# Reordering a kernel's prologue, its third group of maxima, a PSUM bank and one result store

## The chip, the cores and the metric

One core of one Trainium2 chip runs the kernel. The metric is the device time in microseconds (us) of one execution; a kernel's time is the median of its runs.

## The reference

The input is `x`, 2 sequences of 1024 tokens with 256 features. Four residual layers follow one another, each on a layer-normalised `x`:

1. sliding-window attention: 32 heads of 8 features, window 128, softmax over 256 keys, an output product;
2. an FFN, 256 to 1024 to 256 with relu, whose weights are 4-bit codes times a scale per 64 columns, plus a rank-16 product (LoRA); weights are shared with layer 4;
3. a block with q, k, v through causal convolutions of 4 taps and two silus, unit-length q and k, a delta-rule scan over the tokens with an 8x8 state for each head, an output product, then a gated MLP, 256 to 704 to 256;
4. the FFN again.

```python
x = x + attn_a(layernorm(x))          # softmax(q k^T / sqrt(8)) v, window 128
x = x + ffn(layernorm(x))             # relu(x w_up + b) w_down + b, w = (code-7.5)*scale + A B
x = x + attn_b(layernorm(x))          # S = S - beta (S k - v) k^T per token; then silu(gate) * up @ Wdown
x = x + ffn(layernorm(x))
```

## The kernel before

The 1024 tokens are cut into 8 blocks of 128 (both sequences side by side: 256 columns). The program is one stream for each engine, written out by hand and joined by semaphores. Nothing is planned by a tool: the order of calls in each engine's `body` is the order of the work.

**Software pipeline.** `body(t)` works on three blocks at once: block n = t+1 (attention, first FFN and the inputs of layer 3, called `following`), block t (the scan, `scan`) and block s = t-1 (gated MLP and second FFN, `tail`). `front` means that block n+1 is prepared too: its norm, its q and k, its maxima. `body(-1)` has neither scan nor tail, `body(0)` no tail, bodies 1 to 5 have everything, body 6 has no `front`. Then `last_scan` and a body with only a tail.

**Attention.** Each block has 32 units of 2 heads, in four groups (g) of 8. Scores are computed twice: `scores_max` (L1576) makes them in banks 1 and 2 for VectorE's row maxima (`max_unit`, L1053), `max_pieces` splits the maxima into three bf16 pieces, `turn_max` (L1605) transposes them, and ScalarE's `max_rows` (L705) writes them by DMA into the stacked queries. `scores` (L1616) then yields scores less the maximum, `exp_of` (L713) the exponentials, `values` (L1641) the product with v. The stacks (q in three bf16 pieces, k likewise, a row of maxima, a pad row) come from DRAM by SyncE's `load_stacks` (L397), 7 DMAs for a group, in a ring of three slots. For a block, maxima of groups 0 to 2 are made in the body before, those of group 3 in its own attention (`PASS1`, L54), with `turn_max(n, 3)` at unit `TURN_AT` (L59).

**FFN stretch.** After the attention, TensorE has the wo product, gate and up products of block s (`gate_up` L1788, banks 4 and 7 in turn, `late_bank`), the FFN of block n (`ffn_up`, `ffn_down`), the maxima of group 2 of block n+1, then `mlp_down` (L1801), beta and delta inputs of block n (`turn_a(n,3)`, `beta_in`, `delta_in`), and `ffn_c_up`/`ffn_c_down` of block s. VectorE's side: `act_of` (L1315, gate times up) between scan steps, `second_residual` (L1104), the maxima, `second_sums` (L1297, the scan's output, which SyncE stores), `third_residual` (L1324, needs `mlp_down`), convolutions, `products` (L1161), `result` (L1333), which SyncE stores and which frees bank 5 for `values` of the next block. The next body begins with `til_first` (L1180), which waits for three DMAs of q, k and v lanes.

**Prologue.** SyncE, ScalarE and GpSimd each issue loads in the order written. ScalarE has codes, scales and LoRA factors ahead of its first compute. SyncE has the constants, all layer weights, and then the stores of the q and k pieces. VectorE dequantises both FFN weights. TensorE waits for every weight, then makes the maxima of three groups, then enters `body(-1)`.

## Time and profile before

| | us |
|---|---|
| median of 3 runs (lowest, highest) | 1237.23 (1232.9, 1240.89) |
| the profiled execution | 1245.38 |
| its span | 1243.5 |

| engine | busy us | share of the span |
|---|---|---|
| TensorE matmul (PE) | 1010.6 | 81% |
| weight load (PEld) | 720.0 | 58% |
| VectorE (DVE) | 901.1 | 72% |
| ScalarE (ACT) | 520.6 | 42% |
| GpSimd (POOL) | 75.1 | 6% |

Mean granted TensorE clock: 0.904 of full. The chain of work that ended last is 36% DVE, 33% PE, 11% ACT, 7% DMA, 6% issue and 5% SyncE's queue. No engine is full; which of them ends a stage has to be read stage by stage. A busy share says how much of a stretch the engine had something in it, not that it set the end.

### The profile page before, as it was taken

The numbers are of one execution on the slowest core, as the hardware profiler recorded it, in microseconds if no ns is written. First come the engines' busy times: TensorE is split into PE (matmuls) and PEld (weight loads), VectorE is DVE, ScalarE is ACT, GpSimd is POOL, SyncE is SP. The second block draws the span as 40 slices with busy tenths as digits, with TensorE's granted clock in tenths as the row PEclk, the third lists the DMA queues.
The fourth block names the chain that finished last, engine by engine and source line by source line (L and its number), as shares of the span: only waits on it lengthen the run. The fifth ranks groups of instructions, "written<-read, shape, count | busy, mean of one in ns | idle before, by whom it ended". The sixth has DMA issues, their size and how long they took to land.

```text
span 1243.5 us, 24387 instructions
## 1 busy us (share of the span) xinstructions
PE 1010.6 (81%) x9880; PEld 720.0 (58%) x9880; DVE 901.1 (72%) x2297; ACT 520.6 (42%) x1075; POOL 75.1 (6%) x107
## 2 busy tenths in 40 slices
PE   3488778777988998889888997899888978866567
PEld 2256645554566766666666665676665656744445
DVE  2733377897889778887888786977888687967911
ACT  2034255326542655336532663364533644531122
POOL 2200000000000010001000010000000100010000
PEclk9579979986998999989999998999999989987768
DMA  9823013303420144013411242014300300020000
GB/s 281 154 42 75 22 59 82 57 1 96 85 43 1 43 112 75 2 35 95 81 22 35 78 80 40 1 46 110 75 1 27 95 3 1 18 77 1 1 25 9
DMA packets 94129, 67.90 MB, mean 55 GB/s; under 512 B 47744, under 2 KB 86848, under 8 KB 94016
## 3 DMA queue, kind: packets, MB, share of 16 engines
q1 hardware_dynamic: 88544, 60.75, 20.6%
q10 hardware_dynamic: 4960, 5.54, 1.7%
q8 instruction: 78, 1.28, 0.5%
q14 instruction: 35, 0.29, 0.1%
q0 software_dynamic: 512, 0.05, 0.1%
HBM read 45.57 MB, written 20.32 MB: 53 GB/s over the span
## 4 chain that ended last, share of the span: by engine, by line
DVE 36%; PE 33%; ACT 11%; DMA 7%; issue 6%; SPq 5%; POOL 1%; ACTq 0%; DVEq 0%; POOLq 0%
PE bank L1651 5%; PE bank L1805 4%; DVE state L1268 4%; DVE u_l L1255 4%; DVE state L1260 4%; DVE lane_buf L1246 4%; PE bank L1631 3%; PE bank L1748 3%; DMA q_l<-lane_q 3%; DVE lane_buf L351 3%; DVE mx L1056 2%; PE bank L1540 2%; DVE hid L1209 2%; DVE til L1210 2%; PE bank L1599 2%
## 5 line engine op out<-in xcount | busy, mean ns | idle before, releaser
L715 ACT ACTIVATE probs<-bank 128x512 f32<-128x512 f32 x256 | 152.2, 597 | 165.7 <-PE bank L1636 165.1
L1651 PE MATMUL bank<-probs,v_ext 128*9 128x128 f32 x2048 | 165.5, 284 | 16.1 <-ACT probs L715 6.9
L1056 DVE TENSOR_REDUCE mx<-bank 128x2 f32<-128x320 f32 x256 | 118.5, 485 | 53.8 <-PE bank L1599 48.6
L1594 PE MATMUL bank<-edge_mask,identb 128*32 128x128 bf16 x1024 | 81.8, 240 | 63.1 <-DVE mx L1056 43.0
L1796 PE MATMUL bank<-feat_c,wgu 128*128 128x256 f32 (+1 forms) x384 | 100.3, 414 | 26.7 <-DVE hid_c L1321 21.1
L1651 PEld LDWEIGHTS bank<-probs,v_ext 128*9 128x9 f32 x2048 | 91.0, 93 | 44.6 <-issue 21.9
L1631 PE MATMUL bank<-q_stack,k_stack 128*128 128x128 bf16 x1024 | 106.1, 229 | 8.6 <-DMA q_stack<-m_rows 7.9
L1599 PE MATMUL bank<-k_stack,q_stack 128*32 128x160 bf16 x2048 | 108.1, 256 | 0.0
L1796 PEld LDWEIGHTS bank<-feat_c,wgu 128*128 128x128 f32 (+1 forms) x384 | 74.0, 198 | 48.4 <-DVE hid_c L1321 24.7
L1631 PEld LDWEIGHTS bank<-q_stack,k_stack 128*128 128x128 bf16 x1024 | 62.4, 100 | 56.9 <-issue 28.4
L1594 PEld LDWEIGHTS bank<-edge_mask,identb 128*32 128x32 bf16 x1024 | 37.7, 97 | 92.6 <-DVE mx L1056 65.9
L1246 DVE TENSOR_TENSOR lane_buf<-state,til 128x128 f32<-128x128 f32 x256 | 74.7, 292 | 16.6 <-POOL lane_buf L603 10.2
L1268 DVE TENSOR_REDUCE state<-state 128x32 f32<-128x160 f32 x256 | 81.4, 318 | 7.2
L1255 DVE TENSOR_REDUCE u_l<-lane_buf 128x16 f32<-128x144 f32 x256 | 77.1, 301 | 7.0
L1260 DVE TENSOR_TENSOR state<-u_l,k_l 128x128 f32<-128x128 f32 x256 | 74.7, 292 | 7.6
L1723 PE MATMUL bank<-feat,w_up 128*128 128x256 f32 x256 | 66.4, 410 | 5.4 <-ACT feat L677 5.4
L1819 PE MATMUL bank<-feat_c,w_up 128*128 128x256 f32 x256 | 65.5, 406 | 5.1 <-ACT hid_c L861 3.7
L1540 PE MATMUL bank<-w_dn,hid 128*128 128x256 f32 x256 | 59.1, 390 | 8.0 <-ACT hid L780 8.0
L1134 DVE SCALAR_TENSOR_TENSOR conv<-raw,conv_w,conv 128x256 f32<-128x256 f32 x144 | 63.4, 482 | 2.6
L1636 PE MATMUL bank<-tri_mask,identb 128*32 128x128 bf16 x1024 | 62.6, 235 | 0.0
L1599 PEld LDWEIGHTS bank<-k_stack,q_stack 128*32 128x32 bf16 x2048 | 61.9, 103 | 0.6
L1819 PEld LDWEIGHTS bank<-feat_c,w_up 128*128 128x128 f32 x256 | 50.0, 202 | 20.9 <-ACT hid_c L861 6.2
(169 smaller groups left out, 1732.7 us busy)
## 6 DMA issues: line engine op xcount, KB each, us to landing
k_pieces<-conv SPq DMA_DIRECT2D x48, 128.0 KB, 2.3
k_stack<-k_pieces SPq DMA_DIRECT2D x32, 192.0 KB
k_stack<-k_pieces SPq DMA_DIRECT2D x32, 128.0 KB
k_l<-lane_k SPq DMA_DIRECT2D x8, 512.0 KB, 3.7
q_l<-lane_q SPq DMA_DIRECT2D x8, 512.0 KB, 5.7
q_pieces<-conv SPq DMA_DIRECT2D x24, 128.0 KB, 2.0
q_stack<-q_pieces SPq DMA_DIRECT2D x32, 96.0 KB
tok<-in_x SPq DMA_DIRECT2D x8, 256.0 KB, 3.2
```

The lines of the kernel that those rows point to most:

```text
L715: act.activation(probs[:, u % 2], score_bank[u % 2][:], ACT.Exp, scale=float(DK) ** -0.5).then_inc(exp_done, 1)
L1056: dve.tensor_reduce(mx[:, g, 2 * v:2 * v + 2], bank[1 + u % 2][:].rearrange("p (h k) -> p h k", h=2)[:, :, 0:SPAN], AX.X, ALU.max).then_in ...
L1246: at = mark(dve.tensor_tensor(first[:, c, :, :, 0:DK].rearrange("p v i (k e) -> p i v k e", e=2), state[:, c, :, :, C:C + 2].rearrange("p ...
L1255: at = mark(dve.tensor_reduce(u_l[:, c], first[:, c], AX.X, ALU.add))
L1260: at = mark(dve.tensor_tensor(products_of(c), u_l[:, c].rearrange("p v (o i) -> p v o i", o=1).broadcast_to([128, VR, DK, C]), kc[:, c:c + ...
L1268: at = mark(dve.tensor_reduce(state[:, c + 1, :, :, C:C + 2], state[:, c].rearrange("p v k (e j) -> p v k e j", e=2), AX.X, ALU.add))
L1594: pe.matmul(pb[rows].rearrange("p (h e t) -> p h e t", h=2, e=2)[:, :, :, 0:SUB], identb[:, rows], edge_mask[:].rearrange("p (o e t) -> p ...
L1599: last = pe.matmul(pb[s * SUB:(s + 1) * SUB, hp * 2 * W:hp * 2 * W + SPAN], q_stack[:, r, 2 * v + hp, s * SUB:(s + 1) * SUB], keys_of(r, 2 ...
L1631: last = pe.matmul(pb[:, at:at + W], keys_of(r, 2 * v + hp)[:, kb * W:(kb + 1) * W], q_stack[:, r, 2 * v + hp, :], start=(hp == 0 and kb = ...
L1651: last = pe.matmul(bank[5][row:row + VE, col:col + W], v_ext[:, b, kb, h, :], probs[:, u % 2, (hp * 2 + kb) * W:(hp * 2 + kb + 1) * W], st ...
L1796: last = pe.matmul(late_bank[i % 2][0:m, g * BT:(g + 1) * BT], wgu[:, k, g * INTER + 128 * i:g * INTER + 128 * i + m], fc[:, k], start=(k ...
L1819: last = pe.matmul(late_bank[i % 2][:, 0:BT], w_up[:, k, i * 128:(i + 1) * 128], fc[:, k], start=(k == 0), stop=(k == KT - 1))
```

## The change

- **Loads.** Codes and scales go from ScalarE's to SyncE's queue, the up half right behind the constants, the down half behind the pad stores. LoRA factors: up ones on SyncE, down ones on ScalarE. `ones`, `head_sum`, `to_lanes` join the layer weights, and these and `load_residual(0)` come after the stacks, `load_x(1)` and the landing of the first two groups' maxima. q pieces are stored from ScalarE's queue, k pieces from SyncE's; the pad rows are loaded from GpSimd's. Waits for `weights_in` move from the prologue to the first use (`relu_a(0,0)`, the wo product, `delta_weights`).
- **Prologue compute.** TensorE makes the LoRA up product first, ahead of the first transpose. VectorE clears `k_stack` first, dequantises the up weights in the prologue, adds the down part later; ScalarE copies the LoRA down product out of PSUM. The norm weights are multiplied in behind `first_apply(0)`.
- **Third group.** The prologue makes the maxima of groups 0 and 1 only; those of group 2 of block 0 are made in units 2 to 5 of the first attention, two a unit, with `turn_max` at unit 7.
- **Gates.** The six gate tiles use banks 4, 7, 3, 4, 7, 4; tile 2 waits for nothing, tile 3 for act 1, tile 4 for act 2, tile 5 for act 4.
- **Down product.** `mlp_down` is cut by sequence; two maxima tiles, half, two tiles, half, four tiles. VectorE's `second_sums` moves ahead of the last four of these maxima.
- **Small ones.** `TURN_AT` 20 to 19. `result` before `products(n, 1)`. `til_first` waits for the k and v lanes only, ScalarE's `queries_out` for the q lanes.

```diff
-TURN_AT = 20
+TURN_AT = 19
+THIRD_AT = 2
+        gate_bank = (bank[4], bank[7], bank[3], bank[4], bank[7], bank[4])
+        GATE_FREE = {3: 1, 4: 2, 5: 4}
...
@@ SyncE
             load_x(0)
+            for dst, src in [(lora_a_up, a["lora_a_up"]), (lora_b_up, a["lora_b_up"])]:
+                sp.dma_start(dst, src).then_inc(lora_up_in, 16)
             for dst, src in consts:
                 sp.dma_start(dst, src).then_inc(consts_in, 16)
+            quantised(q_up, a["q_up"], s_up, a["s_up"], KT, up_in)
             sp.wait_ge(zeroed, 1)
...
-            load_residual(0)
-            pieces_to_dram(0)
+            quantised(q_dn, a["q_dn"], s_dn, a["s_dn"], FT, dn_in)
+            first_keys()
             sp.wait_ge(pieces_out, 144)
             sp.wait_ge(pad_out, 48)
             sp.wait_ge(stack_init, 2)
             for g in range(RING):
                 load_stacks(0, g)
-                load_pad(0, g)
-            sp.wait_ge(tok_next_ready, 1)
             load_x(1)
+            for g in range(2):
+                sp.wait_ge(m_in[g], 16)
+            load_residual(0)
+            for dst, src in plain:
+                sp.dma_start(dst, src).then_inc(weights_in, 16)
...
@@ GpSimd
+            pool.wait_ge(stack_init, 2)
+            for r in range(RING):
+                load_pad(pool, 0, r, first_pads)
@@ ScalarE, attention
+                    if n == 0 and u == THIRD_AT + 5:
+                        max_rows(0, 2)
@@ VectorE
-                dve.wait_ge(lanes_in, n * 48 + 48)
+                dve.wait_ge(lanes_in, n * 32 + 32)
...
                 if front:
-                    for u in range(2 * UPG + 2, 3 * UPG):
+                    for u in range(2 * UPG + 2, 2 * UPG + 4):
+                        max_unit(n + 1, u)
+                if has_scan:
+                    second_sums(step)
+                if front:
+                    for u in range(2 * UPG + 4, 3 * UPG):
                         max_unit(n + 1, u)
                     max_pieces(n + 1, 2)
-                if has_scan:
-                    second_sums(step)
...
                     products(n, 0)
-                    products(n, 1)
                 if tail:
                     result(s)
+                if following:
+                    products(n, 1)
...
+            zero = mark(dve.memset(k_stack[:], 0.0))
             norm_next_vars(0)
@@ TensorE
+                    if n == 0 and THIRD_AT <= u < THIRD_AT + 4:
+                        for v in range(2):
+                            scores_max(0, 2 * UPG + 2 * (u - THIRD_AT) + v)
...
-                if i >= 2:
-                    pe.wait_ge(act_ready, n * IT + i - 1)
+                if i in GATE_FREE:
+                    pe.wait_ge(act_ready, n * IT + GATE_FREE[i])
...
-                if front:
-                    for v in range(2 * UPG, DONE_EARLY * UPG):
-                        scores_max(n + 1, v)
-                if tail:
-                    mlp_down(s)
+                for b in range(B):
+                    if front:
+                        for v in range(2 * UPG + 2 * b, 2 * UPG + 2 * b + 2):
+                            scores_max(n + 1, v)
+                    if tail:
+                        mlp_down(s, b)
+                if front:
+                    for v in range(2 * UPG + 4, DONE_EARLY * UPG):
+                        scores_max(n + 1, v)
...
+            pe.wait_ge(lora_up_in, 32)
+            for k in range(KT):
+                for c in range(2):
+                    last = pe.matmul(bank[2 * k + c][:], lora_a_up[:, k * 128:(k + 1) * 128],
+                                     lora_b_up[:, c * 512:(c + 1) * 512], start=True, stop=True)
+            last.then_inc(up_prod, 1)
             pe.wait_ge(early_in, 16 * (len(early) + 2))
             turn_next(0)
```

## Rows read from the trace of the kernel before

**Rows 1.** Stretches: us, busy us (instructions) of PE, PEld, DVE, ACT, POOL, granted clock, DMA share, GB/s.

```profile
0.00:40.00 40.00, 20.13 (x54) 13.36 (x55) 17.65 (x15) 8.34 (x14) 12.78 (x19) 0.92 1.05 285
52.00:73.00 21.00, 12.23 (x291) 6.67 (x291) 13.71 (x40) 0.52 (x2) 0.00 (x0) 0.50 0.45 57
```

**Rows 2.** Timeline of the prologue: start us, us, engine, line, operation, count, [idle before, releaser].

```profile
13.42 2.12 ACT L963 COPY wqkv_a<-hid 128x512 f32<-128x512 f32 x2 [11.40 <-issue]
18.73 5.90 PE L1553 MATMUL bank<-feat_c,wqkv_a 128*128 128x256 f32 x16 [0.77 <-ACT feat_c L669]
28.69 5.11 SPq L431 DMA_DIRECT2D k_pieces<-conv  x2
30.23 4.05 PE L1904 MATMUL bank<-hid_c,u_l 16*128 16x512 f32 x8 [0.80 <-ACT v_ext L701]
```

**Rows 3.** Timeline of the prologue: stacks of group 0, first maxima, pieces of group 1, attention.

```profile
41.81 0.33 SPq L400 DMA_DIRECT2D q_stack<-in_zero_rows  x1
52.46 0.30 PE L1594 MATMUL bank<-edge_mask,identb 128*32 128x128 bf16 x4 [11.35 <-DMA k_stack<-in_pad_row]
60.45 0.30 PE L1594 MATMUL bank<-edge_mask,identb 128*32 128x128 bf16 x4 [3.54 <-DMA k_stack<-in_pad_row]
65.48 0.17 DVE L1065 TENSOR_SCALAR mpieces<-mx 128x16 bf16<-128x16 f32 x1
73.57 0.59 PE L1631 MATMUL bank<-q_stack,k_stack 128*128 128x128 bf16 x4 [0.54 <-DMA q_stack<-m_rows]
```

**Rows 4.** GpSimd's groups up to 60 us: line, operation, count, busy us, mean ns, idle before.

```profile
L552 POOL DMA_DIRECT2D k_stack<-k_stack x12 | 6.1, 514 | 0.0
```

**Rows 5.** DMA issues of the whole run: target and source, queue, count, KB each, us to landing.

```profile
q_l<-lane_q SPq DMA_DIRECT2D x8, 512.0 KB, 5.7
sqk<-lane_v SPq DMA_DIRECT2D x8, 256.0 KB, 3.9
```

**Rows 6.** Timeline of body 1: the wo product and gate tile 2, columns as in Rows 2.

```profile
362.83 1.89 PE L1540 MATMUL bank<-wo_a,feat 128*128 128x256 f32 x8
...
373.54 2.61 PE L1796 MATMUL bank<-feat_c,wgu 128*128 128x256 f32 x8 [1.98 <-DVE hid_c L1321]
```

**Rows 7.** Timeline of body 1: the second residual, maxima, sums, down product.

```profile
400.08 0.69 DVE L1110 TENSOR_TENSOR x<-bank,x_in 128x512 f32<-128x512 f32 x1 [0.88 <-PE bank L1540]
402.38 0.24 PE L1594 MATMUL bank<-edge_mask,identb 128*32 128x128 bf16 x4 [1.84 <-DVE mx L1056]
405.52 3.65 PE L1805 MATMUL bank<-wdown_b,hid_c 128*128 128x256 f32 x8
406.89 3.35 DVE L1282 TENSOR_REDUCE k_l<-lane_buf 128x256 f32<-128x3072 f32 x1
413.25 0.69 DVE L1327 TENSOR_TENSOR x<-bank,x 128x512 f32<-128x512 f32 x1 [3.02 <-PE bank L1805]
```

**Rows 8.** Waits of VectorE, 360 to 1030 us: us in total, times, longest.

```profile
DVE x L1327 <- PE bank L1805: 13.9, 5, 3.2
```

**Rows 9.** Timeline of body 0: the first convolution.

```profile
286.61 0.62 DVE L1132 TENSOR_SCALAR conv<-raw,conv_w 128x256 f32<-128x256 f32 x2 [2.01 <-ACT raw L802]
```

**Rows 10.** Waits of TensorE, 128 to 1110 us: us in total, times, longest.

```profile
PE bank L1631 <- DMA q_stack<-m_rows: 6.3, 3, 3.4
PE bank L1651 <- DVE x L1336: 4.8, 5, 1.0
```

**Rows 11.** Timeline of attention in body 1: pieces of group 3, their transpose, two units' scores.

```profile
340.18 0.17 DVE L1072 TENSOR_TENSOR mpieces<-nmx,mpieces 128x16 bf16<-128x16 f32 x1
342.32 0.24 PE L1613 MATMUL bank<-identb,mpieces 128*48 128x128 bf16 x1
343.04 0.40 PE L1631 MATMUL bank<-q_stack,k_stack 128*128 128x128 bf16 x4
343.98 0.40 PE L1631 MATMUL bank<-q_stack,k_stack 128*128 128x128 bf16 x4
```

**Rows 12.** Timeline of body 0: the first work on the lanes.

```profile
189.87 1.95 DVE L1185 SCALAR_TENSOR_TENSOR til<-k_l,beta_l 128x1024 f32<-128x1024 f32 x1 [3.73 <-DMA q_l<-lane_q]
```

More of the change, by code:

```diff
@@ L354, in state_terms, with load_pad @@
                 q_t[:, cs].rearrange("p c (o i) k -> p c o i k", o=1).broadcast_to([128, NC_ // 2, VR, C, DK]), ALU.mult)
+        def load_pad(queue, n, r, landed):
+            for e in range(CHUNK // (2 * W)):
+                queue.dma_start(k_stack[PADROW:PADROW + 1, r, :, 2 * W * e:2 * W * (e + 1)],
+                                a["pad_row"][:, n * W:(n + 2) * W].rearrange("a (o t) -> a o t", o=1)
+                                .broadcast_to([1, KC, 2 * W])).then_inc(landed, 16)
         def x2(n):
@@ L421, in next_stacks, with first_keys, quantised @@
                 if n == 1 and g < RING:
-                    load_pad(1, slot(n, g))
+                    load_pad(sp, 1, slot(n, g), pad_in[slot(n, g)])
+            def first_keys():
+                for p, cast in enumerate((piece1, piece2, piece3)):
+                    sp.wait_ge(cast, 2)
+                    for late in range(2):
+                        sp.dma_start(k_pieces[late, :, :, 2 - p, :, 1 - late].rearrange("h b p t -> p (h b) t"),
+                                     pieces[:, 1, p, :].rearrange("p (a t) -> p a t", t=W)).then_inc(pieces_out, 16)
+            def quantised(codes, q, scales, sc, tiles, landed):
+                sp.dma_start(codes.rearrange("p (k n) -> p k n", k=tiles),
+                             q.rearrange("(k p) n -> p k n", p=128)).then_inc(landed, 16)
+                for half in range(128 // QBLK):
+                    rows = slice(half * QBLK, (half + 1) * QBLK)
+                    src = sc.rearrange("(k h) n -> h k n", h=128 // QBLK)[half:half + 1]
+                    sp.dma_start(scales[rows].rearrange("p (k n) -> p k n", k=tiles),
+                                 src.broadcast_to([QBLK, tiles, src.shape[2]])).then_inc(landed, 16)
             def pieces_to_dram(n):
@@ L973, in _ @@
                 piece_third(0, s)
+            act.wait_ge(piece3, 2)
+            for p in range(3):
+                act.dma_start(q_pieces[0, :, :, p].rearrange("h b p t -> p (h b) t"),
+                              pieces[:, 0, p, :].rearrange("p (a t) -> p a t", t=W)).then_inc(pieces_out, 16)
             act.wait_ge(zeroed, 6)
             values_out(0)
-            act.wait_ge(weights_in, 16 * (len(plain) + IT))
-            for g in range(DONE_EARLY):
+            for k in range(FT // 2):
+                act.wait_ge(dn_prod, k + 1)
+                act.copy(w_dn[:, 2 * k:2 * k + 2, :].rearrange("p a n -> p (a n)"), bank[4 + k][:]).then_inc(lora_kept, 1)
+            for g in range(2):
                 max_rows(0, g)
@@ L1719, in ffn_up @@
             def ffn_up(n, i):
+                if n == 0 and i == 0:
+                    pe.wait_ge(up_ready, 1)
                 if i >= 2:
@@ L1899, in _ @@
             pe.wait_ge(v_done, 1)
-            pe.wait_ge(lora_in, 64)
-            for k in range(KT):
-                for c in range(2):
-                    pe.matmul(bank[2 * k + c][:], lora_a_up[:, k * 128:(k + 1) * 128],
-                              lora_b_up[:, c * 512:(c + 1) * 512], start=True, stop=True)
+            pe.wait_ge(lora_dn_in, 32)
             for k in range(FT):
@@ L1914, in _ @@
             pe.wait_ge(group_rows, 16 * (5 * W // SUB - 4))
-            for u in range(DONE_EARLY * UPG):
-                scores_max(0, u)
-            for g in range(DONE_EARLY):
+            for g in range(2):
+                for u in range(g * UPG, (g + 1) * UPG):
+                    scores_max(0, u)
                 turn_max(0, g)
```

174 lines of the change are left out of this document (100 added, 74 removed).

## The prediction

> **What bounds the kernel now.** I read the stretches first, then the timeline of the first 75 us, then one full body, then the waits of both big engines. Three things are to be seen.
>
> The first 73.57 us are a prologue before the first unit of attention [rows 3]. Up to 40 us the DMA engines are full (share 1.05 at 285 GB/s, some 11.4 MB) while TensorE is busy half the time [rows 1]. Inside it, ScalarE's first compute waits for its own 12 issues of loads: idle 11.40 us, up to 13.42 [rows 2]. SyncE stores the k pieces into full queues, two issues taking 5.11 us [rows 2]. So the stacks are first asked for at 41.81, and the maxima of group 0 start at 52.46, of group 1 at 60.45 [rows 3]. From 52 to 73 us the granted clock is 0.50, the lower level of 1.2 GHz, TensorE busy 12.2 of 21 us [rows 1].
>
> The FFN stretch changes hands. In body 1 TensorE waits 1.98 us for VectorE's first gate product, and then makes gate tile 2 (2.61 us) ahead of the transpose that the FFN needs [rows 6]. Later TensorE waits for maxima (1.84 us), makes the down product behind them, and VectorE waits 3.02 us for that [rows 7].
>
> **The prologue.** ScalarE keeps 4 issues, some 2 us, so its copy can start when the q and k weights have landed. They and x are 1.1 MB, and at 285 GB/s [rows 1] that is 4 us behind issues that end near 2: about 6.2 instead of 13.42, 7.2 us earlier. From that copy to the start of the q and k product were 5.31 us [rows 2], which would put the product at 11.5. But the LoRA up product now stands ahead of the first transpose on TensorE. Its 8 halves took 4.05 us [rows 2]; its factors land near 7, so it ends near 11 at that pace, near 14 at half of it. The early q and k product shows the slow pace: 5.90 us for 16 halves of 256 columns, 369 ns each [rows 2], where 8 of them took 1.89 us, 236 ns each, at 363 us [rows 6]. I take the slow pace. About 1 us of transpose and copy and 4 to 5.9 us of product end q and k near 20, instead of 24.6. That is 5 us.
>
> What SyncE then stores no longer meets full queues: ahead of the k pieces stand 5.8 MB instead of some 10; at 285 GB/s [rows 1] they are through by 20. The Trainium skill ("DMA: Bandwidth & Descriptors", Issuing engines are not separate DMA queues) holds that loads of different issuing engines share the same 16 DMA engines and interleave, so that a second issuer saves only issue time. By that rule moving codes from one queue to another buys nothing in bandwidth, and only the 4 MB postponed do; my sum counts bytes over all queues and agrees. Six k stores and three q stores, at about half a microsecond an issue as on GpSimd's queue [rows 4], last pieces at 22.5: landed at 26.5 instead of 41.8, 15.3 us earlier.
>
> GpSimd's pads are 6 issues of 514 ns behind its 16 others, 12 of them in [rows 4]; with the stacks initialised near 16 they are out by 28, under cover of the stacks, which need until 36. If that cover fails it costs what exceeds 36. The Trainium skill ("SBUF — State Buffer", Who interferes with whom) says that a VectorE operation in a two-port mode locks GpSimd out, and so its descriptor writing. In this trace 12 issues beside VectorE's dequantising kept 514 ns [rows 4], so no lock shows; with one, the pads would come a few us later, still inside that cover.
>
> Group 0 needs 10.65 us from first issue to first tile, group 1 18.64 [rows 3], of which 1.4 were SyncE's pad issues for group 0. So group 1 starts at 26.5 + 17.2 = 43.7, its pieces come 5.0 us later [rows 3], attention at 49.7: 23.9 us earlier. Against that, the first attention takes 8 tiles more: group 1's took 5.03 us for 8 at the lower clock [rows 3], so 4.4 to 5. Postponed loads (4.1 MB, 14.4 us at 285 GB/s) follow from about 50 and precede group 3's stacks on SyncE; those are wanted near unit 8, about 65. I charge 1 us. The moved VectorE work (2.3 us and 4.1 us) falls where it has nothing else; if that cover is gone it costs at most 6.4. **Prologue: -18 us.** Bounds: -10, if SyncE's issues still take 2 us each as in [rows 2] or the third group is paid twice; -23, if LoRA runs at the fast pace and the postponed loads cost nothing.
>
> **Gates.** Tile 2 no longer waits 1.98 us nor runs between wait and transpose: TensorE's FFN could start 1.98 and part of the tile's own time sooner, some 3 us in body 1 [rows 6]. But VectorE reaches the second residual with only 0.88 us of slack [rows 7] and is late itself in bodies 2 to 5; what is late next is the scan. I take -2 in all; bounds 0 and -3 times 6 bodies = -18.
>
> **Down product.** Its first half runs where TensorE waited for maxima. The 5 waits of VectorE for it, 13.9 us [rows 8], should go: -13.9. `second_sums` (3.35 us [rows 7]) now delays the last four maxima and so TensorE's transpose, beta and delta. In bodies 1 to 5 the halves that are gone from behind the maxima pay for it. In body 0, with no down product, VectorE already waits 2.01 us for the raw tile [rows 9]; that wait grows by 3.3. Sum -10.6. Bounds: 0, where the halves run at the lower clock (8 in 3.65 us [rows 7], so 12 in 5.5) and hold tiles 18 and 20 back; -20, where the transpose moves the full 4 us.
>
> **Result sooner.** TensorE's 5 waits for it, 4.8 us [rows 10], go. VectorE waits about 1.1 us for the second FFN before it, and `products(n,1)` ends 1.9 later, still ahead of the pair products that attention reaches at unit 4: -4.8; bounds +5, -5.
>
> **Lanes.** v lands about 1.9 us ahead of q (3.9 after its issue against 5.7 [rows 5]). In body 0 that counts: VectorE waited 3.73 us [rows 12]. In later bodies the next work waits for the pair products, which attention reaches at unit 4, and gains as much as attention does. -2.3; bounds 0, -6.
>
> **Turn at 19.** One unit is 0.94 us, the pieces are ready 2 us ahead of their transpose [rows 11], and the three waits for the row of maxima are 6.3 us [rows 10]: -2.8; bounds 0, -3.
>
> Steady part: -2 -10.6 -4.8 -2.3 -2.8 = **-22.5 us**. With the prologue -40.5. The profiled execution took 1245.4, so 1204.9; it was 8.2 above the median of the runs, so **1197** in their terms.
>
> **Rivals.**
> - Steady part taken back: down halves at half clock and `second_sums` in front of TensorE's next steps, as body 0 shows [rows 9]. For it: the clock did fall in this stretch, since 8 halves took 3.65 us. Against it: the wait of 1.84 us just before them [rows 7] is what the change fills. Then -18 and the small -5: 1214. Chance 0.15.
> - SyncE stays the bound of the prologue: scales and pads of 2 us an issue, keys late by 7 to 10. Only -8 there: 1207. Chance 0.10.
> - More than counted: TensorE's stream without holes keeps the higher level, both upper bounds half reached: 1182. Chance 0.08.
> - The change doesn't do what it says: the bulk load inside the first attention and the third group take back what the prologue gains, and the scan absorbs the rest: 1237. The 11 us of idle before ScalarE's copy speak against it. Chance 0.05.
> - Slower, by the clock: TensorE's work is 33% of the chain, 410 us, at a mean clock of 0.904. The change pulls its work into thinner pieces in the prologue and around maxima. If the mean falls to 0.79, those 410 us become 469, +59 on -40: 1256. It decides from a mean of 0.82 on, where gain and loss cancel. Against it: every step here removes holes. Chance 0.04.
>
> **Numbers.** The forecast has 0.58, its own range 1188 to 1206. Up to the cases at 1182 and 1214 and the bounds of the prologue (5 us worse, 8 better), the range is 1180 to 1223; it leaves out the last two cases and tails. About 1% is what a measurement of this kernel can tell from no change. Faster 0.91, same 0.05, slower 0.04.
>
> **What would show it.** ScalarE's first copy near 6; stacks asked for near 27; first `scores` near 50; group 3's tiles at unit 14 without a DMA wait. No wait of VectorE for the down product in bodies 1 to 5, one longer by 3 for the raw tile in body 0. No wait of TensorE for `result`. It is wrong if the first attention starts after 58, or one of bodies 1 to 5 shortens by less than 2.

## The result, and the profile after

The changed kernel took 1193.8 us (median of 4 runs, 1189.42 to 1197.89), the kernel before 1238.52 beside it (4 runs, 1232.9 to 1240.89): a ratio of 0.9645, 95% interval 0.9587 to 0.9702. The profiled execution of the changed kernel took 1197.73 us with a span of 1195.9, so it stands 3.9 above the median.

The landmarks below are starts of VectorE's own instructions, read off both timelines (after minus before). Block 0's first residual stands in `body(-1)`, that of block n+1 in `body(n)`. They show where the 47.6 us between the two profiled ends came from.

| landmark | before | after | difference |
|---|---|---|---|
| first residual, block 0 | 130.2 | 116.6 | -13.7 |
| first residual, block 1 | 244.4 | 229.5 | -14.9 |
| first residual, block 3 | 500.6 | 480.4 | -20.3 |
| first residual, block 5 | 771.4 | 736.1 | -35.3 |
| first residual, block 7 | 1034.0 | 988.5 | -45.5 |
| last result | 1240.3 | 1192.7 | -47.6 |

So 13.7 us came from the prologue with the first attention, and 33.9 from the steady part. The same timelines split the 33.9: -19.8 in the stretches from second residual to first convolution of bodies 1 to 5, +2.8 in that of body 0, -15.6 between the first convolution and the next first residual, where the lanes, the turn and the result lie, and -1.3 elsewhere.

The stretches of after that answer to [rows 1] (same columns: us, busy us of PE, PEld, DVE, ACT, POOL, granted clock, DMA share, GB/s). The first 40 us move 7.9 MB in place of 11.4:

```profile
0.00:40.00 40.00, 21.91 (x56) 12.81 (x56) 19.89 (x19) 10.80 (x18) 20.18 (x33) 0.92 0.88 197
52.00:73.00 21.00, 17.75 (x303) 11.63 (x304) 10.90 (x28) 7.94 (x17) 0.00 (x0) 0.78 0.73 221
```

The prologue's timeline of after, against [rows 2, 3] (start us, us, engine, line, operation, count, idle before and its releaser):

```profile
5.69 2.14 ACT L991 COPY wqkv_a<-hid 128x512 f32<-128x512 f32 x2 [3.66 <-DMA wqkv_a<-in_wqkv_a]
9.17 7.19 PE L1975 MATMUL bank<-hid_c,u_l 16*128 16x512 f32 x8 [9.17 <-DMA hid_c<-in_lora_b_up]
16.29 1.11 PE L1587 MATMUL bank<-ident,sqk 128*128 128x128 f32 x4
18.17 6.39 PE L1620 MATMUL bank<-feat_c,wqkv_a 128*128 128x256 f32 x16 [0.77 <-ACT feat_c L692]
25.21 3.91 SPq L440 DMA_DIRECT2D k_pieces<-conv  x6
27.35 2.33 ACTq L1004 DMA_DIRECT2D q_pieces<-conv  x3
...
33.96 0.32 SPq L418 DMA_DIRECT2D q_stack<-in_zero_rows  x1
...
42.53 0.30 PE L1661 MATMUL bank<-edge_mask,identb 128*32 128x128 bf16 x4 [8.16 <-DMA k_stack<-k_pieces]
54.68 0.17 DVE L1099 TENSOR_SCALAR mpieces<-mx 128x16 bf16<-128x16 f32 x1
56.91 0.58 PE L1698 MATMUL bank<-q_stack,k_stack 128*128 128x128 bf16 x4 [1.07 <-DMA q_stack<-m_rows]
```

ScalarE's copy starts 7.7 us sooner, as forecast, yet the query/key product ends at 24.56 us, where it ended in the kernel before (24.63, [rows 2]). The gain begins only behind it: the six key stores take 3.91 us, the query stores go out beside them from ScalarE's queue, and the stacks are asked for 7.9 us sooner.

Body 1 of after, against [rows 7], and the convolution of body 0 against [rows 9]. Between second residual and third residual there is no wait left:

```profile
384.86 0.68 DVE L1144 TENSOR_TENSOR x<-bank,x_in 128x512 f32<-128x512 f32 x1
387.84 2.00 PE L1887 MATMUL bank<-wdown_b,hid_c 128*128 128x256 f32 x8
388.86 3.34 DVE L1316 TENSOR_REDUCE k_l<-lane_buf 128x256 f32<-128x3072 f32 x1
394.72 0.68 DVE L1361 TENSOR_TENSOR x<-bank,x 128x512 f32<-128x512 f32 x1
...
275.84 0.62 DVE L1166 TENSOR_SCALAR conv<-raw,conv_w 128x256 f32<-128x256 f32 x2 [2.85 <-ACT raw L830]
```

Waits of after from 128 to 1070 us (us in total, times, longest), VectorE's and TensorE's, against [rows 8, 10, 12]. VectorE's wait at the third residual and TensorE's for the result have left the list. What is new is 7.0 us of the result's addition waiting for the second FFN's product, and the lanes' wait is now for v:

```profile
DVE til L1219 <- DMA sqk<-lane_v: 7.2, 6, 2.5
DVE x L1370 <- PE bank L1911: 7.0, 6, 1.2
PE bank L1698 <- DMA q_stack<-m_rows: 1.6, 2, 1.3
```

The stretch from second residual to first convolution, in bodies 1 and 2 of after (columns as above). The same work takes 13.2 us at a granted clock of 1.00 and 14.8 at 0.88:

```profile
384.90:398.10 13.20, 10.07 (x114) 6.89 (x113) 12.69 (x31) 4.93 (x16) 0.00 (x0) 1.00 0.23 75
512.10:526.90 14.80, 12.05 (x116) 8.34 (x115) 12.79 (x31) 4.93 (x16) 1.41 (x2) 0.88 0.22 72
```

Before, it took 17.1 to 18.3 us in bodies 1 to 5, in windows like these:

```profile
400.00:418.00 18.00, 14.54 (x147) 10.25 (x147) 13.31 (x30) 4.82 (x16) 0.65 (x1) 0.91 0.18 58
532.40:550.40 18.00, 14.40 (x128) 9.97 (x120) 13.04 (x30) 4.59 (x16) 0.17 (x1) 0.81 0.18 59
```

### The profile page after: what moved, and what is told of

Its sections match the earlier page's. It is cut to its first block, busy times and chain, and to the rows that moved or that the text cites. A ratio compares the mean times of both kernels' runs of the same rounds, so it can differ in the third digit from the quotient of the medians.

```text
span 1195.9 us, 24393 instructions
## 1 busy us (share of the span) xinstructions
PE 991.5 (83%) x9880; PEld 711.4 (59%) x9880; DVE 899.3 (75%) x2294; ACT 521.2 (44%) x1079; POOL 76.9 (6%) x113
## 4 chain that ended last, share of the span: by engine, by line
PE 38%; DVE 37%; ACT 9%; DMA 7%; issue 6%; SPq 1%; POOL 1%; ACTq 0%; DVEq 0%
PE bank L1718 5%; DVE state L1302 4%; DVE u_l L1289 4%; PE bank L1831 4%; DVE state L1294 4%; DVE lane_buf L1280 4%; PE bank L1698 4%; PE bank L1911 3%; PE bank L1902 3%; PE bank L1607 3%; DVE lane_buf L362 3%; DVE mx L1090 3%; DVE k_l L1316 2%; PE bank L1703 2%; PE bank L1666 2%
## 5 line engine op out<-in xcount | busy, mean ns | idle before, releaser
L1718 PE MATMUL bank<-probs,v_ext 128*9 128x128 f32 x2048 | 161.3, 279 | 13.8 <-ACT probs L738 9.0
L1879 PE MATMUL bank<-feat_c,wgu 128*128 128x256 f32 (+1 forms) x384 | 96.3, 406 | 16.6 <-DVE hid_c L1355 10.8
L1666 PE MATMUL bank<-k_stack,q_stack 128*32 128x160 bf16 x2048 | 103.5, 248 | 0.0
L1294 DVE TENSOR_TENSOR state<-u_l,k_l 128x128 f32<-128x128 f32 x256 | 74.7, 292 | 7.6
L1607 PEld LDWEIGHTS bank<-w_dn,hid 128*128 128x128 f32 x256 | 50.2, 199 | 24.6 <-ACT hid L808 17.6
```

What stands on the lines that cost most here:

```text
L1294: at = mark(dve.tensor_tensor(products_of(c), u_l[:, c].rearrange("p v (o i) -> p v o i", o=1).broadcast_to([128, VR, DK, C]), kc[:, c:c + ...
L1607: last = pe.matmul(dst[:, b * D:(b + 1) * D], src[0:m, k, b * W:(b + 1) * W], w[0:m, k, :], start=(k == 0), stop=(k == tiles[-1][0]))
L1666: last = pe.matmul(pb[s * SUB:(s + 1) * SUB, hp * 2 * W:hp * 2 * W + SPAN], q_stack[:, r, 2 * v + hp, s * SUB:(s + 1) * SUB], keys_of(r, 2 ...
L1718: last = pe.matmul(bank[5][row:row + VE, col:col + W], v_ext[:, b, kb, h, :], probs[:, u % 2, (hp * 2 + kb) * W:(hp * 2 + kb + 1) * W], st ...
L1879: last = pe.matmul(gate_bank[i][0:m, g * BT:(g + 1) * BT], wgu[:, k, g * INTER + 128 * i:g * INTER + 128 * i + m], fc[:, k], start=(k == 0 ...
```

## The experiments

Twelve kernels, each the changed one with the edit named. The medians are of 4 runs (6 for the last). The half interval of a ratio is 0.3 to 0.6%, so the difference of a median to the changed kernel's 1193.8 is uncertain by some 8 to 9 us (an estimate from these intervals). Only two kernels' intervals lie apart from the changed kernel's: the first and the one of the lanes and the turn. The place of an effect is therefore read from landmarks of the profiled execution. "First exponential" is where attention 0 begins on ScalarE, "residual 0" is the first residual of block 0, which the expectations call that of body 0. No run here was timed directly against the changed kernel; all ratios are to the kernel before, whose median was 1236.6 to 1238.1 in the three series.

| kernel | median | ratio to before (95%) | first exponential | residual 0 | last result |
|---|---|---|---|---|---|
| before | 1238.5 | | 74.7 | 130.2 | 1240.3 |
| changed | 1193.8 | 0.9645 (0.9587 to 0.9702) | 57.8 | 116.6 | 1192.7 |
| down product and sums back | 1212.6 | 0.9770 (0.9728 to 0.9813) | 57.7 | 113.2 | 1207.5 |
| sums back | 1202.1 | 0.9699 (0.9653 to 0.9744) | 56.9 | 117.4 | 1197.9 |
| sums early only with a down product | 1188.0 | 0.9602 (0.9552 to 0.9652) | 57.4 | 118.3 | 1191.1 |
| gate banks back | 1193.0 | 0.9639 (0.9594 to 0.9684) | 57.1 | 112.9 | 1186.0 |
| result back | 1200.3 | 0.9682 (0.9640 to 0.9725) | 56.2 | 112.3 | 1194.3 |
| lanes and turn back | 1208.4 | 0.9760 (0.9725 to 0.9795) | 57.4 | 114.6 | 1206.0 |
| third group in prologue | 1198.7 | 0.9674 (0.9624 to 0.9724) | 62.6 | 121.5 | 1191.2 |
| weights early | 1201.4 | 0.9706 (0.9676 to 0.9735) | 67.7 | 127.1 | 1196.6 |
| LoRA behind queries | 1191.1 | 0.9612 (0.9570 to 0.9654) | 55.6 | 111.8 | 1183.9 |
| down weights late | 1199.8 | 0.9686 (0.9643 to 0.9729) | 56.9 | 117.4 | 1191.1 |
| down weights after rows | 1198.0 | 0.9683 (0.9640 to 0.9727) | 52.1 | 116.4 | 1189.4 |
| all combined | 1193.8 | 0.9645 (0.9612 to 0.9677) | 51.1 | 117.4 | 1189.9 |

Landmarks of a single trace scatter too, and this table shows by how much. Seven kernels share the changed kernel's prologue and first attention (itself and the six of the down product, sums, banks, result and lanes; one has the turn at 20): their residual 0 lies between 112.3 and 118.3. Six share the part behind it, but for when the down weights are scaled (the changed kernel and the five that edit the prologue alone): from residual 0 to the last result they take 1069.5 to 1076.1 us, and the changed kernel is the slowest of them. The kernel before takes 1110.1.

The scatter of residual 0 goes with one wait inside attention 0. TensorE makes the next block's first maxima at unit 25 and may have to wait for their stacks, here in the changed kernel and in the one with sums early only with a down product:

```profile
97.77 0.24 PE L1661 MATMUL bank<-edge_mask,identb 128*32 128x128 bf16 x4 [2.10 <-issue]
99.15 0.30 PE L1663 MATMUL bank<-edge_mask,identb 128*32 128x128 bf16 x4 [4.49 <-DMA k_stack<-k_pieces]
```

In these two and in the kernel with the sums back (2.4 us) the granted clock falls to 0.50 during the wait or about 1 us behind it, for 3.5 to 7 us, and the attention takes 58.8 to 60.9 us. In the other four no such wait is over 1.5 us, the clock stays at 1.00, and it takes 55.5 to 57.2.

**Down product and sums back.**

```
-for b in range(B):  [two maxima tiles]; mlp_down(s, b)
-[four maxima tiles]
+[eight maxima tiles]; mlp_down(s, 0); mlp_down(s, 1)
 ... VectorE: second_sums(step) behind max_pieces(n + 1, 2)
```

> The changed kernel with two of its parts undone: the MLP's down product stands again whole behind the eight maxima tiles of the third group on TensorE, and VectorE's second sums again behind all eight maxima. Theory A (this pair gave the whole shortening between the second residual and the first convolution, 19.8 us over bodies 1 to 5, and cost 2.8 us in body 0): that stretch is 17.0 to 18.0 us long again in bodies 1 to 5 (13.2 in the changed kernel's third body) and 13.3 us in body 0 (16.0), VectorE waits 2.5 to 3 us at the third residual five times, and the whole is 16 to 18 us slower than the changed kernel, about 1211. Theory B (the pair is worth only the wait it removes, 13.9 us, as I predicted, and some other part gave the remaining 6): the stretch returns to 16.0 us and the whole is about 1205 us.

The median is 1212.6, 18.8 us slower, and the two intervals don't meet. The stretch is 17.8, 17.1, 18.5, 17.7 and 18.4 us in bodies 1 to 5, and 13.1 in body 0: theory A. The window of body 1, its down product and the wait behind it:

```profile
377.60:395.30 17.70, 14.09 (x121) 9.90 (x121) 13.03 (x30) 4.82 (x16) 0.41 (x1) 0.81 0.18 60
...
383.35 3.36 PE L1884 MATMUL bank<-wdown_b,hid_c 128*128 128x256 f32 x8
387.70 1.99 PE L1884 MATMUL bank<-wdown_b,hid_c 128*128 128x256 f32 x8
390.79 0.69 DVE L1361 TENSOR_TENSOR x<-bank,x 128x512 f32<-128x512 f32 x1 [2.72 <-PE bank L1884]
```

The same 8 products take 3.36 us and then 1.99: the order of before leaves TensorE idle ahead of the maxima (4.12 us here, up to 379.84), and behind that lull part of the stretch runs at the lower of its two levels (mean granted 0.81). So the pair gives two things: the wait (2.1 to 3.5 us a body) and the level. The price of the level is read in the kernels that keep the pair: the stretch takes 13.2 to 13.8 us at a granted 1.00, 14.7 to 14.8 at 0.88 and 15.4 to 15.9 at 0.78 to 0.80. Which bodies get which level differs from trace to trace of the same code, so the five stretches sum to 67.5 to 75.0 us with the pair (69.1 in the changed kernel), against 88.9 before and 89.6 here.

**Sums back.** Only VectorE's half of that edit.

```
-    [two maxima units]; second_sums(step); [four units]; max_pieces
+    [six maxima units]; max_pieces; second_sums(step)
```

> The changed kernel with the down product still in two halves among the maxima, and only the second sums moved back behind all eight maxima. Theory A (the interleaved product needs the second sums as its cover): VectorE runs out of maxima tiles while TensorE is in a half of the product, about 1.5 us in each of bodies 1 to 5, which gives back 5 to 8 us there; body 0, which has no down product, gets back the 2.8 us. Net 2 to 5 us slower than the changed kernel, about 1198. Theory B (the halves fit into TensorE's lead over VectorE of two banks): no wait in the maxima, bodies 1 to 5 as in the changed kernel, body 0 2.8 us shorter, about 1191.

The stretch takes 15.6 us in each of bodies 1 to 5, and 13.3 in body 0. In body 1 (window, and VectorE's wait inside it):

```profile
384.40:400.00 15.60, 13.15 (x126) 8.95 (x124) 12.78 (x30) 5.26 (x18) 0.00 (x0) 1.00 0.05 19
390.83 1.86 DVE L1090 TENSOR_REDUCE mx<-bank 128x2 f32<-128x320 f32 x4 [2.32 <-PE bank L1663]
```

By the trace this is theory A, a bit larger than expected: with the interleaving alone the granted clock is 1.00 in all five stretches, but VectorE stands 2.32 us for the second half of the product, and that is what the sums cover. The median is 8.3 us above the changed kernel's (the intervals overlap), the last result 5.3 later.

**Sums early only with a down product.**

```
-if has_scan: second_sums(step)            (ahead of the last four maxima)
+if has_scan and tail: second_sums(step)   (behind them otherwise)
```

> The changed kernel with the second sums ahead of the last four maxima only in the bodies that have a down product (1 to 5); in body 0, where none stands among the maxima, they are behind all eight again. Theory A (in body 0 the sums only hold up the maxima, and with them the third turn of tokens): the stretch from second residual to first convolution in body 0 is 13.3 us again (16.0 in the changed kernel), nothing else changes, 2.7 us faster, about 1191. Theory B: what it wins there is lost at the next place where the outputs' round trip is awaited: 1194.

Body 0's stretch is 13.3 us again (261.2 to 274.5), as theory A said. The last result comes 1.6 sooner, although this run's first residual came 1.7 later. The median is the lowest of all, 1188.0, but its interval overlaps the changed kernel's, and from residual 0 to the last result it takes 1072.8 us, within the range of the kernels without this edit. The stretch is shown; a gain of the whole is not.

**Gate banks back.**

```
-gate_bank = (bank[4], bank[7], bank[3], bank[4], bank[7], bank[4]);  GATE_FREE = {3: 1, 4: 2, 5: 4}
+gate_bank = (bank[4], bank[7], bank[4], bank[7], bank[4], bank[7]);  GATE_FREE = {2: 1, 3: 2, 4: 3, 5: 4}
```

> The changed kernel with the gated tiles on two banks again, as before. I had counted 2 us for the third bank; the traces of before and after show only 0.9 us less between the first and second residual in body 1 and nothing (31.8 us in both) in bodies 2 to 5. Theory A (that is all of it): 0 to 1 us slower, about 1194. Theory B (the third bank keeps TensorE busy enough for the later stretches to run at full clock, 1.00 in the changed kernel against 0.81 to 0.91 before): the stretch from second residual to convolution is 1.5 us longer in some bodies, 3 to 6 us slower, about 1198.

The median is 1193.0, no change, and the five stretches stay at 13.2 to 13.8 us with the granted clock at 1.00, against theory B. The third bank is worth less than can be measured.

**Result back.**

```
-products(n, 0); result(s); products(n, 1)
+products(n, 0); products(n, 1); result(s)
```

> The changed kernel with the result's addition again behind both products of the units, not between them. Theory A (as counted in the prediction: TensorE waited 0.8 to 1 us for it at the start of each next attention, five times): 4 to 5 us slower, about 1198. Theory B (after the other changes the result waits for the late product anyway, 7.0 us over six bodies in the changed kernel, so that its place no longer matters): within 1 us, 1194, and the 7.0 us of waiting of VectorE shrink, since the products stand ahead of it.

It is 6.5 us slower by the median (the intervals overlap), 1.6 by the last result. TensorE's wait for it is back with the same numbers as in [rows 10] (128 to 1070 us), as theory A said:

```profile
PE bank L1717 <- DVE x L1370: 4.8, 5, 1.0
```

Theory B is right in part: VectorE's 7.0 us of waiting for the product are gone, but its waits for v's lanes rise from 7.2 to 12.2 us. The stretches from first convolution to next first residual in which the wait lies are 0.7 to 1.1 us longer in four of five cases, and 1.5 shorter in the fifth. The mechanism is shown, its size is not.

**Lanes and turn back.**

```
+dve.wait_ge(queries_in, n * 16 + 16)      (in til_first)
-TURN_AT = 19
+TURN_AT = 20
```

> The changed kernel with the first step of each body's triangular solve waiting for all three lane transfers again, the queries' among them, and the fourth group's turn at unit 20 in place of 19. Theory A (as counted in the prediction, 2.3 and 2.8 us, with one of the two hiding part of the other): 3 to 5 us slower, about 1198, and the solve's first step starts 0.4 us later in each body. Theory B (both lie beside other work): the stretches from first convolution to the next first residual stay at 81.4 to 82.9 us, within 1 us, 1194.

It is 14.6 us slower, far more than either theory said, and the intervals lie apart. VectorE's whole wait ahead of the solve is 24.8 us in 8 bodies (this view gives it as "issue"), against 7.2 in the changed kernel and 28.4 for q's lanes in the one before, whole run:

```profile
  issue: 24.8, 8
```

```profile
DVE til L1185 <- DMA q_l<-lane_q: 28.4, 8, 4.7
```

In body 1, for instance:

```profile
300.53 1.99 DVE L1220 SCALAR_TENSOR_TENSOR til<-k_l,beta_l 128x1024 f32<-128x1024 f32 x1 [3.01 <-issue]
```

```profile
299.32 1.99 DVE L1219 SCALAR_TENSOR_TENSOR til<-k_l,beta_l 128x1024 f32<-128x1024 f32 x1 [1.36 <-DMA sqk<-lane_v]
```

So 17.6 us of waiting come back. By the landmarks 9.9 us are lost between the first convolution and the next first residual, and 3.2 in the stretches from second residual to first convolution of bodies 1 to 5, where the level is lower in this trace (0.88 in four of them against two), which may be chance. TensorE's wait for the rows of maxima stays as small with the turn at 20 as at 19 (1.7 and 1.6 us, 6.3 in [rows 10]). The run does not separate the two edits; the waits speak for the lanes.

**Third group in the prologue.**

```
-within attention 0, units 2 to 5: two tiles of group 2 each; turn_max and max_rows at unit 7
+for g in range(3): [eight tiles]; turn_max(0, g)      (in the prologue)
```

> The changed kernel with the third group's eight maxima tiles back in the prologue, before the first attention, instead of within it. Theory A (they wait there for group 2's stacks and then cost their 4.7 us in full, while inside the attention VectorE does them in about the same 4.7 us but without waiting for the stacks): the first attention starts 6 to 8 us later (about 56 in the changed kernel), it is 4 to 5 us shorter, and the first residual of body 0 comes 2 to 3 us later: about 1196 us. Theory B (the move only shifts the work): first residual within 1 us, 1194. Theory C (inside the attention they cost more than 5 us, since they hold TensorE's units back): first residual earlier, 1190.

The median is 4.9 us slower, the intervals overlap. Residual 0 is 4.9 us later, and so was the first exponential: the attention did not get shorter without the eight tiles (58.9 us, 58.8 with them). But it runs at a lower mean clock, over these windows of this kernel and the changed one:

```profile
62.60:121.50 58.90, 53.18 (x850) 35.61 (x849) 18.12 (x48) 26.53 (x49) 0.00 (x0) 0.88 0.50 125
```

```profile
57.70:116.50 58.80, 53.64 (x952) 37.16 (x949) 22.26 (x59) 26.78 (x50) 0.00 (x0) 0.94 0.58 138
```

The granted clock is 0.50 for the first 6.9 us of the attention here and for 3.4 there, and its later fall lasts 6.8 us here and 3.5 there. So this pair does not price the tiles. The pair with the same course of the clock is the kernel before (0.50 for 3.1 us, a fall of 3.5 us) and the changed one: their first attentions take 55.6 and 58.8 us, so the tiles cost some 3 us, an estimate from one trace each. I had charged 4.4 to 5. That the tiles bring a sooner rise is not shown: the kernel before has none of them there and rises as soon.

**Weights early.**

```
 quantised(q_dn, ...)
+for dst, src in plain: ...;  for i, m in inner: ...   (18 loads)
 first_keys()
```

> The changed kernel with the eighteen postponed loads (the other projections' weights and constants) issued ahead of the first key pieces again, as in the kernel before. Theory A (the order of the loads is what the prologue's gain is made of): SyncE issues about 9 us of loads first and the key pieces queue behind them, the stacks are asked for at 41 to 43 (33.96 in the changed kernel, 41.81 before), the first exponential at 64 to 67 (57.8), the first residual of body 0 6 to 8 us later; about 1202. Theory B (the first stacks wait for the cold TensorE products and GpSimd's pad rows, not for loads): under 2 us later, 1195.

The stacks are asked for at 43.26 (33.96), the first exponential is 9.9 us later, residual 0 10.5 later, and the median 7.6, with overlapping intervals. Residual 0 is 8.8 us beyond the latest of the seven above, so this is theory A by the trace: the order of the loads is the larger part of the prologue's gain.

**LoRA behind queries.**

```
-[LoRA up product]; turn_next(0); queries_keys; ... values_in
+turn_next(0); queries_keys; ... values_in; [LoRA up product]      (VectorE adds it after both scalings)
```

> The changed kernel with the prologue's LoRA up product (8 products, 7.19 us at half clock, from 9.17) moved behind the first queries, keys and values, in front of the LoRA down product. Theory A (this product holds up the transpose of x, which VectorE has ready at 10.0 but which starts at 16.29): the query/key product starts at 12 and ends at 18.5 (24.56), the key pieces are issued from 19.5 (25.21), the stacks of group 0 are asked for at 28 (33.96), its first tile runs at 36.5 (42.53), and the first attention starts 5 to 6 us earlier: about 1188 us. Theory B (the loads are the bound: 88% of the transfer time of the first 40 us is busy, and the pieces' writes and the stacks queue behind the quantised weights): the product ends at 18.5, the first tile is not before 40, gain under 2.5 us, about 1192. Theory C (the two LoRA products one after the other, 11 us, are now the last to be ready): first tile at 40 to 42 behind the wait for the up weights, gain 0 to 2 us.

```profile
12.05 6.49 PE L1624 MATMUL bank<-feat_c,wqkv_a 128*128 128x256 f32 x16 [0.77 <-ACT feat_c L692]
19.18 8.65 SPq L440 DMA_DIRECT2D k_pieces<-conv  x6
24.14 3.69 PE L1995 MATMUL bank<-hid_c,u_l 16*128 16x512 f32 x8 [0.80 <-ACT v_ext L724]
27.68 6.75 PE L2000 MATMUL bank<-u_l,hid 16*128 16x256 f32 x16
31.87 0.32 SPq L418 DMA_DIRECT2D q_stack<-in_zero_rows  x1
```

Both A and B are half right. The product ends at 18.54, 6.0 us sooner: the LoRA product did hold it. But the six key issues now take 8.65 us in place of 3.91, into the loads of the down weights (the transfers have a share of 1.17 from 18 to 28 us), and the stacks are asked for only 2.1 us sooner. Residual 0 at 111.8 is 4.8 us before the changed kernel's, but only 0.5 before the earliest of the seven with its prologue, and the median gains 2.8: neither is a gain beyond the scatter.

**Down weights late.** The same, and the quantised down weights behind the stacks.

```
-quantised(q_dn, ...); first_keys()
+first_keys(); ... [stacks]; load_x(1); quantised(q_dn, ...)
```

> The changed kernel with the LoRA up product behind the first values (as in the run before) and, besides, the quantised down weights and their scales loaded behind the first three stacks and the next tile, in place of ahead of the key pieces; VectorE scales them after the third group's maxima. In the run with the LoRA product alone the query/key product ended 6.0 us sooner (18.54), but the six key issues then took 8.65 us in place of 3.91 and the stacks were asked for only 2.1 us sooner (31.87), the first tile ran at 40.7. Theory A (the loads ahead of the pieces held them): key issues take about 4 us again, stacks asked for near 26, first tile at 35 (then bound by the LoRA down product, which ends at 34.5), first exponential at 50 (55.6), the whole 4 to 6 us faster than with the LoRA move alone, about 1186. Theory B (the round trip of the pieces and the pad rows on GpSimd's queue hold it, whatever else is loaded): first tile not before 39, gain under 2 us, about 1190. Theory C: the down weights come too late for VectorE within the first attention, some us are lost again at the first residual of body 0.

The stacks are asked for at 26.14, but the row maxima of group 0 then queue behind the down weights: attention 0's first scores

```profile
56.06 0.59 PE L1702 MATMUL bank<-q_stack,k_stack 128*128 128x128 bf16 x4 [6.74 <-DMA q_stack<-m_rows]
```

Group 0's rows were issued at 43.54 (the 49.65 in the next expectation is group 1's issue; TensorE's wait is for group 0's). The transfers have a share of 1.07 from 49 to 56 us. What was won is lost at this wait: the first exponential is at 56.9 (57.8). The median of 1199.8 meets neither theory's number (1186, 1190) and is not distinct from the changed kernel's; the last result is 1.6 us sooner.

**Down weights after rows.**

```
+sp.wait_ge(m_in[0..1], 16); quantised(q_dn, ...); load_residual(0); [weights]
+VectorE: down_scaled(); down_weights() behind first_apply of block 0
```

> The changed kernel with the LoRA up product behind the first values, and the quantised down weights and scales loaded only when the row maxima of groups 0 and 1 have landed; VectorE scales and adds them between the first apply and the delta weights of body 0. In the run before, where these loads stood right behind the stacks, the stacks were asked for at 26.1 and the last maxima of group 1 ended at 48.7, but the transfer of the row maxima, issued at 49.65, landed only at 56.9 among them (TensorE waited 6.7 us), and the first attention began no sooner than in the changed kernel (56.9, 57.8). Theory A (that collision took the whole gain): TensorE waits under 2 us for the row maxima, the first exponential is at 50 to 51, the first residual of body 0 at 109 to 111 (116.6), the whole 5 to 7 us below the changed kernel, about 1188. Theory B (the transfers are saturated through the first attention too, 1.0 and more of the 16 engines' time from 64 to 80 us): the loads that come later push the next stacks and the weights for the attention's output, the first residual is at 113 to 117, gain under 3 us.

Now the first scores run at 51.18, 5.7 us sooner than in the changed kernel, and residual 0 is still at 116.4. Attention 0 meets the next wall (its wait and the windows around it):

```profile
83.82 0.30 PE L1665 MATMUL bank<-edge_mask,identb 128*32 128x128 bf16 x4 [7.47 <-DMA k_stack<-k_pieces]
...
60.00:76.00 16.00, 15.98 (x195) 10.21 (x189) 2.36 (x9) 8.56 (x16) 0.00 (x0) 1.00 1.09 317
76.00:84.00 8.00, 0.53 (x16) 0.24 (x14) 0.00 (x0) 0.60 (x2) 0.00 (x0) 0.83 0.96 138
84.00:92.00 8.00, 8.00 (x176) 5.75 (x168) 4.25 (x12) 3.50 (x7) 0.00 (x0) 0.74 0.47 103
```

This is theory B: the transfers are full from 60 to 76 us with the postponed weights, and group 3's stacks stand behind them. The median is 1198.0, with an interval that overlaps the changed kernel's.

**All combined.** These prologue edits, with the sums early only with a down product.

> All that the runs point to in one kernel: LoRA up product behind the first values, down weights loaded after the row maxima of groups 0 and 1 and scaled behind the first apply, second sums ahead of the last maxima only in bodies with a down product. If the parts add up: 5 to 7 us from the prologue and 2.7 us from body 0, 8 to 10 us below the changed kernel, about 1185. If the prologue's gain is lost again in the first attention (theory B of the run with the down weights after the row maxima): 1189 to 1191.

The median of 6 runs is 1193.75, no better than the changed kernel. Body 0's stretch is short again (13.3 us) and the first exponential at 51.1, but TensorE waits 9.6 us for group 3's stacks. The version for which the runs speak is the changed kernel with the sums moved in body 0 only (1188.0); that it beats the changed kernel beyond the uncertainty is not shown.

## Why the prediction came out, step by step

The forecast was 1197 (1180 to 1223), the measured time 1193.8. The total is near in part by luck, since its two halves err to opposite sides: prologue -18 predicted, -13.7 found; steady part -22.5 predicted, -33.9 found. In terms of the profiled execution the forecast was 1204.9 and 1197.7 was measured, so it is 7 us off there; I took the profiled execution to be 8.2 us above the median, and for the changed kernel it was 3.9. The traces of the kernels that share a part put the prologue's gain at 11.9 to 17.9 us and the steady part's at 34 to 41, each against the one trace of before.

**Prologue: the failed step is "q and k near 20".** ScalarE's copy came as forecast (5.69 for 6.2). The LoRA product's factors landed at 9.17, not near 7, and its 8 halves took 7.19 us, so it ended at 16.4, not near 14. The "near 14" was also a slip: 7 us and twice 4.05 make 15.1. One product took 1056 ns (median) here against 587 in the kernel before at 30 us, and 587 again when moved to 24 us. So q and k ended at 24.56, 4.6 us late. The last piece was issued at 29.7, 5.1 us behind that where I had 2.5, and landed 4.3 us later where I had 4: the stacks were asked for at 33.96 and not at 26.5. SyncE's two scale issues did take 7.03 us, but they ended at 18.0, ahead of the key pieces, and held no store up. From the stacks on the count was right: the first scores came some 23 us behind them, as forecast (23.2). The pad rows went out by 31.7 us, ahead of the stacks, so their cover held. That no lock shows beside VectorE's dequantising says little, since no row shows in which mode it ran.

The mechanism holds (moved away, the product ends 6.0 us sooner), but it is not the only bound: with LoRA and down weights out of the way the stacks are asked for at 26.1, which was my number, and the gain is then lost at the row maxima, or at group 3's stacks when the down weights come later. My 1 us for the postponed loads against group 3's stacks holds for the changed kernel, where their tiles at 80.95 wait for nothing. It fails once attention starts 6 us sooner with the down weights among these loads: 7.5 us. The rival in which SyncE stays the bound was thus about half true: keys late, by pieces that stand behind the LoRA product and not by slow scale issues. Against this, the first attention grew by 3.2 us, where I had charged 4.4 to 5 for the third group and 1 for the loads.

**Gates: -2, found 0.** Body 1's first to second residual became 0.9 us shorter in the traces (33.0 to 32.1), and it is 32.1 with the banks back as well, so this is not the banks' doing; the undone edit changed nothing. VectorE is late itself, as the bound of 0 had it.

**Down product: -10.6, found -17.0** in the traces (19.8 us over bodies 1 to 5, less 2.8 in body 0, predicted 3.3), +18.8 by the median when undone. Over all traces with the pair it is -11 to -19, by the level that they met. The wait of 13.9 us [rows 8] went; the rest is the clock. I had the row in hand, 8 halves in 3.65 us [rows 7], where the next 8 took 1.99 in the same trace, and used it only as a bound against the change:

```profile
410.16 1.99 PE L1805 MATMUL bank<-wdown_b,hid_c 128*128 128x256 f32 x8
```

Removing the lull gave back the level as well: 1.00 in three of five bodies. In body 0 the loss was of the right size but not in the forecast place: the wait for the raw tile grew from 2.01 to 2.85 us only, since VectorE makes the sums ahead of it.

**Result sooner: -4.8**, found 6.5 by the median and 1.6 by the profiled end when undone, with the wait of 4.8 exactly back. The runs agree with the forecast and do not sharpen it.

**Lanes and turn: -5.1, found -14.6** by the median when undone, 9.9 in the stretches where they act. This is the largest relative miss. I used one row, body 0 [rows 12], and argued that later bodies are paced by the attention. The waits before stood in every body: 28.4 us in eight, 3.73 in body 0; after, 7.2. The change cut 21.2 us of VectorE's waiting, and part of that was time. The 2.8 us for the turn show in no wait: with the turn back at 20 the wait for the row of maxima stays at 1.7 us.

**The rivals.** "Steady part taken back" is excluded: its loss in body 0 is there (2.8 us) and stays there. "More than counted" came true in the steady part alone. "The change doesn't do what it says" is excluded by the interval. The fall of the clock did not come; the mean rose from 0.904 to 0.926.

## What to carry to other kernels

Take a wait from a view of the whole run, not from one body: a row of 3.73 us in one body was 28.4 us in eight. When a wait of TensorE goes, price the clock too, at the durations of the same product on either side of the lull. Before a landmark's difference is called an effect, read the same landmark in every trace that shares the code up to it: here they differed by 6 us. A load postponed out of a full stretch must be followed to the next transfer that somebody waits for; here three different orders of the loads moved the wait from key pieces to row maxima to the fourth group's stacks, and none brought residual 0 clearly ahead.

## What the runs showed of the hardware

The first products of the program ran slowly while the clock column read 1.00: the LoRA up product took 1056 ns for one at 9 to 16 us, against 587 ns at 24 us in another run of the same work. Where the column does fall, to 0.50 from 28 us on in that other run, the LoRA down product took 629 ns for one from 27.7 to 34.4 us, against 374 in the changed kernel ahead of its fall at 33.9. So at the very start the durations, not the column, tell the pace.

From some 25 to 34 us on, the granted clock is 0.50, the level of 1.2 GHz, until the first attention runs: it rises to 2.4 GHz 2.7 to 6.9 us behind the first exponential in all fourteen traces (at 61.2 us in the changed kernel, at 69.5 in the one with the third group in the prologue). In nine of them it falls again inside the attention, during or about 1 us behind a wait of TensorE of 1.8 to 9.6 us (in the kernel before, 2.1 us up to 111.49 and the fall at 111.9). In the five without a fall the longest such wait is 2.1 us.

Issues on SyncE's queue take longer when the transfers are full: the same six stores of key pieces took 8.65 us at a share of 1.17 (18 to 28 us, LoRA behind queries) and 3.31 us at 0.62 (17 to 22 us, down weights late).
